# A graph network on one core: products of zeros ahead of the edge products, one more source tile on ScalarE, and layer 0's own terms behind a tile

## What is computed

```python
h = maximum(layernorm(x), 0)
xs = [h]
for W, b in layers 0, 1, 2:
    m = concatenate([h[dst], h[src] - h[dst]]) @ W + b      # per edge
    h = relu(segment_sum(m, dst) / maximum(count(dst), 1))
    xs.append(h)
x = x + concatenate(xs) @ Wf + bf
h = maximum(layernorm(x), 0) @ W4
agg = segment_sum(edge_weight * h[src], dst) + bias
x = x + relu(batchnorm(agg) * gamma + beta)
```

## Time and profile before

| | |
|---|---|
| median of 3 runs | 110.76 us (110.75, 110.76, 111.12) |
| the profiled execution, its own time | 111.02 us |
| its span, first to last instruction | 108.9 us |
| busy | PE 98.9, weight loads 92.0, DVE 87.4, ACT 64.2, POOL 20.8 us |

### The profile page before, as it was taken

How to read it: one execution, slowest core, us unless ns; L and a number is a source line. 1 busy time by engine, 2 the same in 40 slices (tenths; PEclk the granted TensorE clock), 3 DMA queues, 4 the chain that set the end, 5 groups by cost and what they waited for, 6 DMA issues and landing times.

```text
span 108.9 us, 2713 instructions
## 1 busy us (share of the span) xinstructions
PE 98.9 (91%) x1049; PEld 92.0 (84%) x1049; DVE 87.4 (80%) x255; ACT 64.2 (59%) x156; POOL 20.8 (19%) x27
## 2 busy tenths in 40 slices
PE   0297999989999999999999999999999999999950
PEld 0334899977799989999999999999999999999840
DVE  2489999999999998999954599931999989708960
ACT  1497999999699988312958034557413154423540
POOL 7200000000000069000499920192000000000000
PEclk9999999999999999999999999999999999999999
DMA  1846791000120000000051100000000000000026
GB/s 27 251 80 132 182 303 40 0 9 0 14 88 0 6 6 3 6 0 3 7 185 41 61 0 0 6 0 0 0 6 0 0 0 0 0 0 6 0 75 163
DMA packets 7009, 4.63 MB, mean 43 GB/s; under 512 B 2175, under 2 KB 6994, under 8 KB 6994
## 3 DMA queue, kind: packets, MB, share of 16 engines
q1 hardware_dynamic: 6068, 3.68, 12.4%
q10 hardware_dynamic: 926, 0.75, 2.5%
HBM read 3.79 MB, written 0.64 MB: 41 GB/s over the span
## 4 chain that ended last, share of the span: by engine, by line
PE 78%; DVE 8%; ACT 7%; DMA 3%; issue 1%; DVEq 0%; SPq 0%; ACTq 0%
PE bank L1392 14%; PE bank L1293 14%; PE bank L1149 12%; PE bank L1150 11%; PE bank L1151 11%; PE bank L1223 4%; DMA edge_rows_i<-in_dst_dram 3%; PE bank L1430 3%; PE bank L1370 2%; PE bank L1212 2%; DVE stats L544 2%; ACT u_hi L922 1%; PE bank L1190 1%; DVE stats L864 1%; PE bank L1475 1%
## 5 line engine op out<-in xcount | busy, mean ns | idle before, releaser
L590 DVE TENSOR_SCALAR src_hot<-node_id,edge_cols 125x626 f16<-125x626 f16 x77 | 23.6, 376 | 0.0
L1293 PEld LDWEIGHTS bank<-dst_hot,src_hot 125*128 125x128 f16 x505 | 18.9, 98 | 2.1 <-DVE src_hot L590 0.7
L1293 PE MATMUL bank<-dst_hot,src_hot 125*128 125x84 f16 (+6 forms) x505 | 20.0, 196 | 0.5 <-DVE src_hot L590 0.3
L1392 PE MATMUL bank<-counts,u_lo 125*128 125x312 f32 (+3 forms) x60 | 16.7, 309 | 0.0
L1075 ACT ACTIVATE h_hi<-pre 128x312 fp32r<-128x312 f32 (+1 forms) x12 | 5.6, 467 | 16.4 <-DVE pre L757 16.4
L1392 PE MATMUL bank<-counts,u_hi 125*128 125x312 f32 (+3 forms) x48 | 14.1, 307 | 0.0
L1149 PE MATMUL bank<-wf_hi,h_hi 128*125 128x256 f32 x40 | 11.2, 281 | 0.0
L1151 PE MATMUL bank<-wf_lo,h_hi 128*125 128x256 f32 x40 | 11.2, 281 | 0.0
L1150 PE MATMUL bank<-wf_hi,h_lo 128*125 128x256 f32 x40 | 11.2, 281 | 0.0
L1392 PEld LDWEIGHTS bank<-counts,u_lo 125*128 125x128 f32 (+1 forms) x60 | 11.0, 189 | 0.0
L1010 ACT ACTIVATE parts<-bank 125x250 f32<-125x250 f32 x25 | 10.3, 414 | 0.0
(11 more groups left out here) (144 smaller groups left out, 250.4 us busy)
## 6 DMA issues: line engine op xcount, KB each, us to landing
raw<-in_L_gnn_W_dram SPq DMA_DIRECT2D x3, 512.0 KB, 6.4
x_in<-in_x_dram ACTq DMA_DIRECT2D x1, 560.0 KB
raw<-in_L_gnn_Wf_dram SPq DMA_DIRECT2D x1, 512.0 KB, 3.8
out_dram<-x_in SPq DMA_DIRECT2D x2, 168.0 KB
wf<-in_L_gnn_Wf_dram SPq DMA_DIRECT2D x1, 256.0 KB, 7.4
raw<-in_L_gnn_Wf_dram SPq DMA_DIRECT2D x1, 256.0 KB, 2.7
raw<-in_L_gnn_W_dram SPq DMA_DIRECT2D x1, 256.0 KB, 2.6
out_dram<-x_in SPq DMA_DIRECT2D x2, 112.0 KB
```

The costliest lines, as they stand in the source:

```text
L590: dve.tensor_scalar(src_hot[:, t % RING, 0:IDS], node_id[:, 0:IDS], edge_cols[:, 0, t:t + 1], None, ALU.is_equal).then_inc(src_hot_vector, 1)
L1293: return pe.matmul(built[s][:, :, n0:n0 + n], src_hot[:, t % RING, BLK * s:BLK * s + P], dst_hot[:, c, :, j // 2, c0:c0 + n, j % 2], start ...
L1392: ins = pe.matmul(bank[KF * h + f][:, 0:e - a], u[0:n, k, P * f:P * (f + 1)], counts[0:n, k, a:e], start=False, stop=(k == NB - 1 and u is ...
```

## The change

1. Ahead of the wait for the edges PE does eight products of zeros with zeros, 512 columns each, into bank 4, as soon as DVE has cleared `zeros_bf` (new semaphore `zeros_ready`). The products behind the parts are 12 instead of 9.
2. Source tile 57 is made by ACT in block 1, not by DVE (DVE makes 76).
3. ACT copies own terms 1 to 3 behind tile 52 instead of ahead of it, so its order in block 1 is: (1,4), tile 52, own terms 1 to 3, tile 57, `wb_hi`, block (2,0).
4. `h0_hi` is copied in one instruction for both halves, and POOL waits for it once.
5. Seven waits of ACT go that other waits or the order cover.

```diff
-SCALAR_EARLY, ... SCALAR_LATER = (0, 4), (22, 27), {0: (34, 38), 1: (52,), 2: (71,)}
+SCALAR_EARLY, ... SCALAR_LATER = (0, 4), (22, 27), {0: (34, 38), 1: (52, 57), 2: (71,)}
...
@@ POOL
+            pool.wait_ge(h0_hi_ready, 1)
             for f in range(KF):
-                pool.wait_ge(h0_hi_ready, f + 1)
                 pool.tensor_tensor(h0_lo[:, f, 0:NODES], ...
@@ DVE
-            dve.memset(zeros_bf[:, :], 0.0)
+            dve.memset(zeros_bf[:, :], 0.0).then_inc(zeros_ready, 1)
@@ ACT
             act.wait_ge(rel_ready, 1)
-            groups.wait_filled(act, "edges")
             copy(edge_cols[:, :, :], ...
             groups.wait_filled(act, "parts")
-            act.wait_ge(padding_ready, 1)
...
             act.wait_ge(edge_cols_ready, 1)
-            act.wait_ge(constants_ready, 3)
-            act.wait_ge(padding_ready, 1)
...
-            act.wait_ge(row_signs_ready, 1)
             for r in range(NB):
                 for s in range(NB):
                     copy_block(r, s)
                     if r == 0 and s == 4:
-                        act.wait_ge(penalty_ready, 1)
                         high_rows(("u", 0, 4), 4)
-                    if r == 1 and s >= NB - 2:
-                        if s == NB - 2:
-                            act.wait_ge(vecs_loaded, 16 * 6)
-                        own_terms(0, (0,) if s == NB - 2 else (1, 2, 3))
+                    if r == 1 and s == NB - 2:
+                        act.wait_ge(vecs_loaded, 16 * 6)
+                        own_terms(0, (0,))
                 for t in SCALAR_LATER.get(r, ()):
                     if t >= RING:
                         act.wait_ge(*last_half(t - RING))
                     source_tile(t)
+                    if r == 1 and t == SCALAR_LATER[r][0]:
+                        own_terms(0, (1, 2, 3))
...
                 if r == 3:
-                    act.wait_ge(h0_t_ready, NB)
-                    for f in range(KF):
-                        copy(h0_hi[:, f, 0:NODES], h0_t[:, f, 0:NODES]).then_inc(h0_hi_ready, 1)
+                    copy(h0_hi[:, :, 0:NODES], h0_t[:, :, 0:NODES]).then_inc(h0_hi_ready, 1)
@@ PE
+            pe.wait_ge(zeros_ready, 1)
+            for _ in range(8):
+                pe.matmul(bank[4][:, :], zeros_bf[:, :], zeros_bf[:, :].unsqueeze(1).to_broadcast([EP, 4, P]),
+                          start=True, stop=True)
             pe.wait_ge(constants_ready, 2)
             pe.wait_ge(edge_rows_ready, 1)
...
-            keep_warm(9)
+            keep_warm(12)
```

More of the change, by code:

```diff
@@ L64 @@
 FULL = 112
-SCALAR_EARLY, SCALAR_NEXT, SCALAR_LATER = (0, 4), (22, 27), {0: (34, 38), 1: (52,), 2: (71,)}
+SCALAR_EARLY, SCALAR_NEXT, SCALAR_LATER = (0, 4), (22, 27), {0: (34, 38), 1: (52, 57), 2: (71,)}
 SCALAR_TILES = SCALAR_EARLY + SCALAR_NEXT + sum(SCALAR_LATER.values(), ())
@@ L292, in gnn_kernel @@
         padding_ready = sem("padding_ready")
+        zeros_ready = sem("zeros_ready")
         row_high_ready = sem("row_high_ready")
```

## The result

| | before | after |
|---|---|---|
| median of 6 runs each, us | 110.75 (110.67 to 111.12) | 111.99 (111.45 to 112.33) |
| profiled execution, us | 111.02 | 111.79 |
| its span, us | 108.9 | 110.0 |
| mean granted clock over the span | 1.000 | 0.984 |

The ratio is 1.009 (95% interval 1.0063 to 1.0117), so the change makes the kernel slower by about 1 us; the medians differ by 1.24 us. All six executions of the changed kernel have a mean granted clock of 0.984 or 0.985. Those of the kernel before lie between 0.990 and 1.000 in all 120 executions taken beside the experiments, on four chips.

The account below looks back on a forecast made before the run. PE was taken as the bound from 28.65 to 98 us. +0.01 (tile 57 and `dev`) - 0.05 (clock at the edges) = -0.04 us, so 110.7 us against the median, range 110.3 to 111.1.

Parts of the forecast that it names:

- the price of the idle time: Before the first transpose: twelve products end earlier, PE waits longer for `h0` at 10.90 us; no gain and no cost.
- rival 3: Clock falls in PE's pause before 10.90 us, slowing the eight products at 12.85: +1.5 us, 112.2 us; chance 0.05.
- The path of the loss: If the clock fell: eight products +1.97 us, less 0.5 of PE's tile waits before the joint at 22.4 us.
- The clock at the edges: Edge and parts products may run at the high clock: 0 to -0.27 us, taken as -0.05 mean over executions.
- rival 4: PE's first product comes at 1.3 us or later, not 1.05, delaying the edges; at 1.9, +0.65 us; chance 0.04.
- rival 5: Products of zeros don't count as work for the clock; front as before, 110.75 us; chance within the forecast's 0.62.
- The stall at `dev`: Ahead of block 2, PE's product `dev` waits for ACT's own term 1: 0.16 us, bounds 0.10 and 0.25.
- The waits for DVE: PE loses 0.15 us waiting for DVE's last tile, 84; with tile 57 off DVE this wait goes.
- the sum of the middle: Tile 57 off DVE and the stall at `dev` together: +0.01 us, the stall taking what the tile gave.
- The copy of `h0_hi`: One ACT instruction instead of two taking 1.42 us, ahead of a pause of 0.43 us: zero effect.
- ACT's lateness after tile 57: ACT copies block (2,0) 0.32 us late, at 31.37 instead of 31.05 us; absorbed, with 0.07 us to spare.

Follow-up runs that it names:

- after: The changed kernel with all five parts of the change, against the kernel before: median 111.99 us, ratio 1.009.
- front_only: Kernel before plus only the eight products of zeros ahead of the edges and twelve instead of nine behind the parts: 111.63 us, ratio 1.0063.
- warm22: Changed kernel with 22 instead of 12 products behind the parts: 110.70 us, ratio to the kernel before 0.9987.
- fill_gap: Changed kernel with eight more products in PE's idle time before the first transpose: 110.51 us, ratio to the kernel before 0.9978.
- mid_only: Changed kernel without the products of zeros and with nine instead of twelve behind the parts: 110.57 us, ratio to the kernel before 0.9983.
- mid_only_2: Repeat of mid_only: 110.78 us, ratio to the kernel before 0.9974.
- fill_gap_2: Repeat of fill_gap: 110.70 us, ratio to the kernel before 0.9959.

## Why the prediction was wrong

The forecast was 110.7 us (110.3 to 111.1), no change; the time is 111.99.

**The step that failed** is the price of the idle time, in the part on twelve products instead of nine: "PE waits longer for `h0` at 10.90 [...]: no gain". It was priced as free. The wait grew from 0.69 to 2.28 us, a little beyond the 1.6 to 2.2 that was forecast, and it brought the clock down: with the gap open 6 of 6 and 10 of 12 executions fell (`after`, `front_only`), with it filled 0 of 12 each (`warm22`, `fill_gap`). That is rival 3, which had a chance of 0.05. Its condition, a fall ahead of the products at 12.85 us, was right. Its price of +1.5 us at the joint agrees with the +1.44 measured by luck: it had +1.97 in the eight products less 0.5 of tile waits, and the runs show +0.99 in them, because the clock was back near 14.9 us, +0.45 ahead of them, and nothing taken back. The chance was wrong because the only row that bore on it, 0.69 us of idleness without harm, says nothing about three times as much, and an unknown of that size was treated as unlikely. The Trainium skill, TensorE: Matmul & The Clock Gate (Why this matters for your kernels), warns of idle gaps between bursts of products. The trace agrees in kind: the clock fell behind a gap of 2.28 us. The page speaks of longer gaps than the 2.15 and 2.28 us that were enough here, and the measurement decides.

**The path of the loss** was only half seen. I had PE itself late and its tile waits taking 0.5 us of that. What happened is that the transposes of blocks 3 and 4 stand behind the eight slow products, and ACT, which makes tile 34 at the joint, waits 1.35 us for them, so the tile is late by as much as PE.

**The clock at the edges** (taken as -0.05, bound -0.27): in the profiled execution -0.23, near the bound; over executions about -0.1 by the two same-chip pairs, which is inside their intervals. Taking the rise as coming 5.3 us after the first product was wrong as a fixed distance: here it came by 4 us. In the eleven traces with the front it came between 4.7 and 6.6 us in eight and between 9.6 and 10.5 in three; in the six without it, between 8.5 and 10.6 us, counted from the start of the span.

**The zeros are late** (rival 4): no, the first product began at 0.99 us and the edges weren't delayed. **The zeros don't count** (rival 5): they do, the clock was up at 5.04 us, only 0.55 us after the first other product, where before it took some 5.3.

**The stall at `dev`** was put at 0.16 us and measured 0.35. The tile costs ACT 1.56 us at this place and not 1.47 (the changed kernel's own terms begin 1.56 us after tile 52 does), and the handover to `dev` took about 0.15 us and not 0.05; bank and order were right. **The waits for DVE** were also short: beside the one at tile 84 (0.15) the kernel before has one of 0.17 us at tile 69, the last of block 3: that block's 141 placings take 5.39 us before and 5.20 in `mid_only`. The two errors cancel, and the sum of the middle, +0.01 us, was measured as -0.04 in the traces. The medians of `mid_only` and `mid_only_2` are 0.25 and 0.17 us under before, more than that. In the trace of `mid_only` the edges start 0.20 us sooner, because the transfer had landed sooner; whether a dropped wait or another part does that over executions was not tested and stays open.

**The copy of `h0_hi`**, one instruction of 1.33 us for 1.42, is hidden as expected. ACT's lateness after tile 57 was put at 0.32 us and is 0.38, counted from the joint; it reaches nobody, since block 3 follows block 2 without a pause.

## What to carry to other kernels

Work that only keeps TensorE's clock up must reach to the next real work. If it ends earlier because the clock is now high, the idle time it leaves can bring the clock down again in the middle of the bounding chain; size filler by the time at which its successor is ready, at the high clock, and look at the granted clock slice by slice. Filler sized so ends late when the clock rises late, as the 112.43 us in `fill_gap_2` shows; four products here kept the clock as well as eight did. A wait that vanishes from one place of a nearly balanced pipeline mostly reappears at the next: measure from joint to joint before counting a gain.

## What the runs showed of the hardware that was not expected

The fall comes late: in the changed kernel the idle time ended at 10.50 us and the clock was still high for about a microsecond of work, then low until near 14.9 us in spite of PE being busy from 12.0 on. The time lost (1.44 us) was three to four times the lead at the first transpose (0.40), of which the clock had given 0.23. The same program falls in some executions and not in others (10 of 12, 8 of 12), and the mean granted clock of an execution tells which: 0.976 to 0.985 against 0.99 or more. The granted clock reads 1.00 in stretches ahead of the first rise, where 512 columns take 0.427 us, so there only the distances between products tell the level.
